# One more attention head of each pair turned by way of memory, and a mask made one slot later

## What is computed

```python
def _L0_gnn_ref(...):
    for l in range(3):
        scores = leaky(si[:, :, None] + sj[:, None, :] + attn_b[l])     # 512 x 512 a graph
        attn = softmax(where(mask, scores, -inf))
        h = layernorm(x + attn @ x, g1[l], beta1[l])
        x = layernorm(h + gelu(h @ W1[l] + b1[l]) @ W2[l] + b2[l], g2[l], beta2[l])

def _L1_gnn_ref(...):
    xh = (x @ W_proj) split into 8 heads of 32
    att = softmax(where(A > 0, leaky(a_src[:, None] + a_dst[None, :] + b_att), NEG_INF))
    out = relu(att @ xh)                                                # for each head

x = _layernorm(x + _L0_gnn_ref(x, adj, ...))
x = _layernorm(x + _L1_gnn_ref(x, adj, ...))
```

## Time and profile before

| | |
|---|---|
| median of 3 runs | 2312.28 us (2310.47 to 2312.49) |
| the profiled execution | 2312.53 us |
| its span | 2310.8 us |
| PE busy | 2213.7 us, 96% |
| DVE busy | 1809.3 us, 78% |
| ACT busy | 1684.7 us, 73% |
| POOL busy | 201.1 us, 9% |

### The profile page before, as it was taken

One profiled execution on the slowest core, in us unless ns is written; L12 is line 12 of the kernel. 1 busy time (PEld: TensorE's weight loads), 2 busy tenths in 40 slices (PEclk: granted clock), 3 DMA queues, 4 the chain that ended last, 5 costly groups with the idle time before them and its releaser, 6 DMA issues.

```text
span 2310.8 us, 32320 instructions
## 1 busy us (share of the span) xinstructions
PE 2213.7 (96%) x10501; PEld 1560.7 (68%) x10501; DVE 1809.3 (78%) x5722; ACT 1684.7 (73%) x3243; POOL 201.1 (9%) x200
## 2 busy tenths in 40 slices
PE   5999999999999999999999999999999999999976
PEld 3766767767766777676676667766776776777643
DVE  5566687878788788887788797887878877766777
ACT  2444468777877768777787778787787877888786
POOL 0010110010100110001100101000100011001100
PEclk9999999999999999999999999999999999999978
DMA  6011025333172242432353430632415322200111
GB/s 221 10 37 55 10 96 158 106 115 124 28 219 87 74 142 78 155 124 65 109 154 97 137 119 29 203 107 73 135 53 184 110 64 93 69 19 19 37 42 37
DMA packets 115874, 219.30 MB, mean 95 GB/s; under 512 B 7768, under 2 KB 57212, under 8 KB 110332
## 3 DMA queue, kind: packets, MB, share of 16 engines
q1 hardware_dynamic: 115708, 217.24, 29.8%
HBM read 164.52 MB, written 52.69 MB: 94 GB/s over the span
## 4 chain that ended last, share of the span: by engine, by line
PE 79%; DVE 13%; ACT 4%; issue 2%; POOL 1%; DMA 0%; DVEq 0%; POOLq 0%; ACTq 0%
PE ffn L1246 22%; PE av L1163 14%; PE ffn L1235 12%; PE av L1235 12%; PE pT L1146 9%; PE av L1187 4%; PE av L1222 2%; DVE prob L778 2%; DVE prob L769 1%; ACT xs L553 1%; POOL rstd L470 1%; DVE lone L730 1%; PE trow L1125 1%; PE av L1273 1%; PE trow L1273 1%
## 5 line engine op out<-in xcount | busy, mean ns | idle before, releaser
L1246 PE MATMUL ffn<-w_sb,G 128*128 128x256 f32 x3072 | 740.5, 381 | 0.0
L1246 PEld LDWEIGHTS ffn<-w_sb,G 128*128 128x128 f32 x3072 | 560.8, 191 | 90.2 <-issue 24.3
L778 DVE CUSTOM_DVE_ANT_0 prob<-trow,mask 128x512 f32<-128x512 f32 x676 | 439.0, 685 | 34.3 <-PE trow L1125 19.5
L1146 PEld LDWEIGHTS pT<-ident,prob 128*128 128x128 f32 x2032 | 256.4, 144 | 147.6 <-issue 101.5
L1235 PE MATMUL ffn<-hT,w_sb 128*128 128x512 f32 x768 | 355.0, 595 | 0.9 <-issue 0.9
L1235 PE MATMUL av<-hT,w_sb 128*128 128x512 f32 x768 | 353.8, 593 | 0.0
L470 POOL TENSOR_TENSOR rstd<-veps,mhalf 128x4 f32<-128x4 f32 x127 | 167.2, 1317 | 2071.9 <-DVE veps L713 2071.9
L513 ACT ACTIVATE prob<-prob,s 128x512 f32<-128x512 f32 x484 | 331.5, 715 | 2.4 <-DVE nm L785 1.8
L1146 PE MATMUL pT<-ident,prob 128*128 128x128 f32 x2032 | 312.3, 278 | 19.8 <-DVE prob L841 7.5
L519 ACT ACTIVATE prob<-prob,nm 128x512 f32<-128x512 f32 x448 | 317.6, 712 | 0.0
L1163 PE MATMUL av<-xs,prob 128*128 128x257 f32 x1024 | 244.3, 380 | 3.9 <-ACT prob L524 3.9
(11 more groups left out here) (154 smaller groups left out, 2727.2 us busy)
## 6 DMA issues: line engine op xcount, KB each, us to landing
w_sb<-in_L_gnn_W SPq DMA_DIRECT2D x48, 1024.0 KB, 8.4
blocks_dram<-blocks SPq DMA_DIRECT2D x168, 256.0 KB, 4.2
prob<-blocks_dram SPq DMA_DIRECT2D x42, 1024.0 KB, 4.8
trow<-rows_dram SPq DMA_DIRECT2D x127, 256.0 KB, 3.2
adj_sb<-in_adj SPq DMA_DIRECT2D x16, 1024.0 KB, 7.0
xin<-in_x SPq DMA_DIRECT2D x16, 512.0 KB, 6.2
x0r<-in_x SPq DMA_DIRECT2D x16, 512.0 KB, 5.8
out<-o SPq DMA_DIRECT2D x15, 512.0 KB, 3.2
```

Source lines behind the costliest of these rows:

```text
L778: return v.tensor_tensor_reduce(out=out_[:, t, :], in0=targets, in1=mask[:, t, :], scale=1.0, scalar=LEAST, op0=ALU.add, op1=ALU.max, accu ...
L1146: last = te.transpose(pT[bank][:, j * P:(j + 1) * P], src[:, t, j * P:(j + 1) * P], ident[:])
L1246: last = te.matmul(ffn[part][:, at:at + D], G[:, f, t * P:(t + 1) * P], w2_sb[:, g // 2 % STAGES, f, :], start=f == 0, stop=f == FT - 1)
```

## The change

`BY_BLOCKS` gets head 6 of every pair, and `AHEAD` gets slot 3. In slot 3 PE now turns head 7 in place of head 6 among the first products (`turned_first`), and nothing among pieces 6 to 9. `moved` now stops at head 107, so heads 97, 98, 100, 101, 102, 104 and 106 go by way of memory too: with the six heads 6 of the earlier pairs, 13 heads more. In slot 3 the two state transposes stand behind piece 13 instead of behind piece 11 (`states_behind`), on PE and likewise for their copies on ACT, and `attend_heads`, `head_rows` and `heads_back` of four heads stand at the unit's end (`spent_last`), as they did in slot 4. `make_masks(0)` goes from slot 3 to slot 4, at the same position among that slot's instructions, and SP's load of the second adjacency, which waits for it, from slot 4 to slot 5.

```diff
-BY_BLOCKS = (1, 2, 4, 5, 8, 10, 13)
-AHEAD = (2, 4)
+BY_BLOCKS = (1, 2, 4, 5, 6, 8, 10, 13)
+AHEAD = (2, 3, 4)
...
 def moved(q):
-    return q < LAST_HEADS - 2 * HEADS and q % (2 * HEADS) in BY_BLOCKS
+    return q < LAST_HEADS - SIDE and q % (2 * HEADS) in BY_BLOCKS
...
 def turned_ahead(g):
-    return [q for q in turned(g)[1:2] if moved(q) and g % SLOTS in AHEAD]
+    return [q for q in turned(g) if moved(q)][:1] if g % SLOTS in AHEAD else []
 
 
 def turned_behind(g):
 
-    return [q for q in turned(g)[1:] if moved(q) and q not in turned_ahead(g)]
+    return [q for q in turned(g) if moved(q)][len(turned_ahead(g)):]
+
+
+def turned_first(g):
+
+    return [q for q in turned(g)[:2] if not moved(q)][:1]
+
+
+def spent_last(g):
+
+    return side_by_side(turned(g))[0] == 2 or g % SLOTS == 3 and side_by_side(turned(g))[0] == 1
...
+def states_behind(g):
+
+    return 3 if spent_last(g) and side_by_side(turned(g))[0] == 1 else 1
...
@@ -423,13 +438,13 @@
+                if k == SLOTS - 1 and not last:
+                    sp.wait_ge(s_masks, 2 * p + 3)
+                    load_adj(2 * p + 3)
                 for q in turned_behind(g)[:1]:
                     move(q)
...
-                if k == SLOTS - 2 and not last:
-                    sp.wait_ge(s_masks, 2 * p + 3)
-                    load_adj(2 * p + 3)
...
@@ -1059,7 +1074,7 @@
-                if k == 3 and p < PAIRS - 1:
+                if k == 4 and p < PAIRS - 1:
                     make_masks(0)
...
@@ -1316,7 +1331,7 @@
-                        for q in heads[:1]:
+                        for q in turned_first(g):
                             turn(q, f - T)
...
-                        if not moved(q):
+                        if not moved(q) and q not in turned_first(g):
                             turn(q, t)
...
-                    if t == 0 and place == 1:
+                    if t == 0 and place == 1 and not spent_last(g):
                         attend_heads(four)
-                    if t == 1:
+                    if t == states_behind(g):
                         for dt in range(DT):
                             transpose_state(s2, dt)
-                    if t == 2 and place == 1:
+                    if t == 2 and place == 1 and not spent_last(g):
                         heads_back(four)
-                if place == 2:
+                if spent_last(g):
                     attend_heads(four)
                 piece(14)
...
-                if place == 2:
+                if spent_last(g):
                     heads_back(four)
```

## The result

The changed kernel takes 2286.03 us (median of 5 runs, 2284.17 to 2287.85) against 2312.28 before (5 runs, 2310.41 to 2313.61): ratio 0.9888, 95% interval 0.9875 to 0.9902. The profiled execution took 2284.84 us, 27.7 less than that of before.

What follows compares the result with a forecast made beforehand. PE was taken as the bound (busy 2213.7 of 2310.8 us, 79% of the chain), DVE next. Slot 3 10.4, slot 4 5.5 and last pair but one 11.5 sum to 27.4: 2312.4 - 27.4 = 2285.0 us, range 2282 to 2292.

Steps and rivals of the forecast that it cites:

- Slot 3: Unit 9 of six pairs: PE loses four turns of a head, 1.74 us each, 10.4 us in all.
- The cover of 2.38 us: Unit 9: DVE's idle time ahead of the attention hides head 6's 2.31 us transpose, by 0.07.
- The margin for the state: Unit 9: normalised state there at 452.30, 0.7 us before PE's transposes ask at 452.98; no wait.
- the sum of landings: Unit 9: head 6's transfers take 4.2 and 4.8 us, landing at 448.2; 5.6 us left for the issues.
- Slot 4: Unit 10 of six pairs: without the mask's lateness on DVE the first wait goes, 0.92 us each, 5.5 in all.
- The second wait: Unit 10: PE's wait for the state before its transposes stays, 1.24 us.
- 0 with 0.76 as the bound: Unit 11: DVE's second addition comes 0.76 us later; cost on PE taken as 0, upper bound 0.76.
- First pair: Units 3 and 4 swap their times, 41.72 and 39.23 us; 0 in sum, bounds -2.5 and +2.5.
- Last pair but one: Units 43 to 46: seven heads leave PE, saving 4.01, 3.48, 3.48 and 0.50 us, together 11.47.
- The first: Rival: DVE or POOL takes part back in slots 3 to 5; 2295 or 2287.5 us, middle 2290; chance 0.22.
- The second: Rival: POOL's shift ahead of its DVE neighbour in slot 4 saves 1.06 us seven times, 2277.6; chance 0.04.
- The fourth rival: Slower: DVE bounds units 10 to 11, the mask's 6.55 us pushing unit 11; 39 us lost, 2324; chance 0.03.

Runs made afterwards that it cites:

- both halves with piece 12: Changed kernel with the mask cut in two between slots 3 and 4, and slot 4's state transposes behind piece 12 instead of 11; 2292.16 us.
- slot 4 in another order: Changed kernel with slot 4 on PE and ACT reordered: two turns, piece 12 and the state transposes, then the other two turns; 2285.4 us.
- all three together: Changed kernel with slot 4's new order, the mask cut between slots 3 and 4, and DVE's first-pair mask work held back in units 2 to 4; 2276.32 us.
- DVE held back: Changed kernel with DVE's mask work in units 2 and 4 of the first pair starting only when the normalised state is written; 2281.86 us.

## Why the prediction was right

**Slot 3.** 1.74 forecast, 1.76 measured; 1.71 for one head in unit 45 alone. The cover of 2.38 us took the transpose's 2.31, with 0.16 us of idle time left where 0.07 was forecast: the transpose's record starts 0.08 us ahead of the end of the one before it, which that subtraction left out. The margin for the state was 0.65 (0.7). SP issued head 6's way back at 445.79 and it landed 4.75 us later, at 450.53; PE asked for it at 453.74. That is 3.2 us of margin, where the sum of landings alone left 5.6; the four issues on the way out, which the prediction left unpriced, took most of the other 2.4.

**Slot 4.** 0.92 forecast, 0.91 measured, and by the mask's move alone as well. Choosing the cadence (30.74 against 29.82) over the printed 0.65 was right. The second wait stayed at 1.09. DVE's lateness behind the mask is there, 0.57 us more into unit 11 than before (0.76 forecast), and costs nothing; the order of slot 4 that added 0.88 to it paid 0.71 for it. So taking 0 with 0.76 as the bound was right, but this cover was nearly spent.

**First pair.** The swap came: 41.95 and 39.23 for 41.72 and 39.23, +0.2 us. The wait of 2.46 us went with the mask from unit 3 to unit 4 in the mask's move alone too (39.23 and 40.26), though there without the lower clock, which came in unit 6 instead (41.45 for 39.76). The prediction took the wait and the lower clock for one thing, and this is the part that came out by luck: of the eleven kernels here that have the wait of 2.46 us, four pay for the clock in unit 6. The sum hardly feels it, since each kernel pays once in units 3 to 6.

**Last pair but one.** 4.01, 3.48, 3.48 and 0.50 forecast, 4.02, 3.45, 3.46 and 0.45 measured.

**Rivals.** The first would have had to show in unit 9 or 11 and did not; the prediction gave it 0.22 for covers that were thin, and the traces found each of them thin but whole. The second asked for POOL's shift to come earlier in slot 4. POOL of the changed kernel in units 9 and 10:

```profile
449.75 0.20 POOL L490 TENSOR_TENSOR shift<-nmean,rstd 128x4 f32<-128x4 f32 x1
...
493.29 1.26 POOL L490 TENSOR_TENSOR shift<-nmean,rstd 128x4 f32<-128x4 f32 x1
```

They took what the earlier trace rows show. The Trainium skill, page SBUF — State Buffer, section "Who interferes with whom", has a GpSimd instruction blocked by a DVE instruction that it shares a port pair with and that was issued first. The trace agrees in where POOL ends: the shift of 1.26 us ends at 494.55, and DVE's `graph_sum`, which starts just before it, at 494.49; beside the block transpose it took 0.20. On who was first the inverse deviation disagrees: in the run with the mask in two halves it had started 1.69 us before the comparison and still ended with it, after 2.94 us instead of 1.91. The fourth rival needed DVE's 5.71 us of idle time in unit 10 to be unusable; the mask used it.

The sum matched better than its parts were known: the traces differ by 27.7 us and the medians by 26.3, and the last unit alone lies between 163.2 and 166.3 us in the profiled executions of these kernels. An agreement within 1 us says no more than that no term of 1 us a pair is missing.

## What to carry to other kernels

Two moves that each load the same engine at the same place must be priced together: here one was worth 5 us alone and 16 beside the other, since it cleared the place that the other filled. To find what a wait costs, compare the time from a common point to the end of the same work in two places, not the idle time printed (0.91 against 0.65). Before moving an instruction out of a wait, look at what stands in order behind the producer: a wait taken from PE came back larger through ACT's queue and its buffer.

## What the runs showed of the hardware

**When the clock falls.** I had taken the lower clock in the first pair as belonging to the wait of 2.46 us that POOL's delay brings to unit 3 or 4. In the traces of before, of after and of five others that wait is followed by it (PE busy 39.3 to 39.5 us instead of 37.8), and the wait of 1.97 us in unit 6 is not. In four others (the mask's move alone, the last pair but one alone, both halves with piece 12, slot 4 in another order) the wait of 2.46 us goes without, and unit 6 pays, for its wait of 1.97. Units 4 and 6 of the mask's move alone, and unit 6 of the changed kernel:

```profile
205.18:245.44 40.26, 37.79 (x157) 27.00 (x156) 27.44 (x91) 16.42 (x24) 4.32 (x3) 1.00 0.17 54
288.08:329.53 41.45, 39.48 (x157) 28.18 (x156) 32.85 (x112) 25.53 (x45) 5.02 (x5) 0.96 0.40 134
...
288.35:328.12 39.77, 37.79 (x157) 27.00 (x156) 32.85 (x112) 23.84 (x40) 5.03 (x5) 1.00 0.42 139
```

So the fall doesn't follow from the length of the wait alone. The wait of 2.38 us in unit 2 was followed by it in all eleven kernels that have it. With units 2 to 4 kept short it came in unit 6 in one kernel (all three together) and in neither place in the other (DVE held back). What decides is open. It costs 1.5 to 1.7 us wherever it comes.

**POOL beside DVE.** The same instruction over 128x4 elements took 1.91 us, 2.41 beside DVE's copy of a mask and 2.94 beside its comparison; another took 0.20 or 1.26. That is up to a microsecond each, on a path where PE waits for the result. A block transpose and a reduction on DVE at the same time went with the short shift of 0.20.
